# Narrow layers: the rests of two units in one transpose, and an accumulation left open for a step

## The reference

```
q = x @ Wq;  k = context @ Wk;  v = context @ Wv        (B: x * rsqrt(mean(x*x) + eps) * norm_w ahead of Wq)
logits = q k^T * scale (+ column bias in A)
x = x + softmax(logits) @ v @ Wo (+ bo in A)
```

## Time and profile before

| | |
|---|---|
| median of 3 runs (lowest to highest) | 2020.38 us (2019.39 to 2020.8) |
| the profiled execution, own time | 2020.28 us |
| its span | 2018.5 us |
| granted TensorE clock | 1.000 of full speed |
| PE, DVE, ACT, POOL busy | 1993.4, 1434.6, 985.6, 646.2 us |

### The profile page before, as it was taken

One profiled execution on the slowest core, in us unless ns is written; L12 is line 12 of the kernel. 1 busy time (PEld: TensorE's weight loads), 2 busy tenths in 40 slices (PEclk: granted clock), 3 DMA queues, 4 the chain that ended last, 5 costly groups with the idle time before them and its releaser, 6 DMA issues.

```text
span 2018.5 us, 31330 instructions
## 1 busy us (share of the span) xinstructions
PE 1993.4 (99%) x11482; PEld 1738.1 (86%) x11482; DVE 1434.6 (71%) x2488; ACT 985.6 (49%) x1814; POOL 646.2 (32%) x518
## 2 busy tenths in 40 slices
PE   8999999999999999999999999999999999999998
PEld 8999988888888887888888888888888878888887
DVE  4423367777777767888888677776777677888886
ACT  3222255444544554655555454444455555555553
POOL 0000043222222255554444332222222354443441
PEclk9999999999999999999999999999999999999999
DMA  8789742222222223343333332222222232333332
GB/s 236 150 174 212 188 92 63 78 62 62 67 78 63 65 75 96 103 112 98 89 100 96 82 111 66 62 67 78 62 63 70 79 89 72 100 95 87 86 74 85
DMA packets 262538, 191.02 MB, mean 95 GB/s; under 512 B 197522, under 2 KB 199986, under 8 KB 259826
## 3 DMA queue, kind: packets, MB, share of 16 engines
q1 hardware_dynamic: 262386, 189.03, 36.8%
HBM read 132.66 MB, written 56.26 MB: 94 GB/s over the span
## 4 chain that ended last, share of the span: by engine, by line
PE 50%; issue 31%; POOL 13%; DVE 4%; ACT 1%; SPq 0%; DMA 0%; POOLq 0%; DVEq 0%; ACTq 0%
POOL prob L1405 6%; PE acc_bank L900 6%; PE ctx_bank L270 4%; PE t_bank L878 4%; PE ctx_bank L271 4%; PE ctx_bank L272 4%; POOL x_s L1380 4%; PE q_bank L856 3%; PE q_bank L858 3%; PE q_bank L860 3%; PE acc_bank L270 3%; PE acc_bank L272 3%; PE acc_bank L271 3%; PE s_bank L270 2%; POOL rest L1414 2%
## 5 line engine op out<-in xcount | busy, mean ns | idle before, releaser
L1405 POOL TENSOR_TENSOR prob<-prob,rinv 128x1232 f32<-128x1232 f32 x128 | 288.3, 2252 | 1010.4 <-DVE rinv L1255 1010.4
L856 PE MATMUL q_bank<-x_s,w_s 128*128 128x512 f32 x768 | 315.6, 411 | 0.8 <-POOL w_s L1398 0.8
L860 PE MATMUL q_bank<-x_s,w_s 128*128 128x512 f32 x768 | 307.1, 400 | 0.0
L858 PE MATMUL q_bank<-x_s,w_s 128*128 128x512 f32 x768 | 307.0, 400 | 0.0
L270 PE MATMUL acc_bank<-o_s,w_s 128*128 128x512 f32 x752 | 304.5, 405 | 2.2 <-DVE o_s L1246 2.2
L272 PE MATMUL acc_bank<-o_s,w_s 128*128 128x512 f32 x752 | 294.4, 392 | 0.0
L271 PE MATMUL acc_bank<-o_s,w_s 128*128 128x512 f32 x752 | 293.4, 390 | 0.0
L1069 ACT ACTIVATE s_bank<-bias_s 128x308 f32<-128x308 f32 x256 | 109.9, 430 | 361.2 <-DVE prob L1217 361.2
L1213 DVE TENSOR_REDUCE mx<-s_bank 128x4 f32<-128x308 f32 x512 | 241.6, 472 | 61.5 <-PE s_bank L272 49.3
L900 PE MATMUL acc_bank<-pT_s,vals_s 128*128 128x512 f32 x1024 | 280.4, 393 | 3.5 <-DVE pT_s L1232 3.5
L1084 ACT ACTIVATE prob<-prob,rstd 128x308 f32<-128x308 f32 x256 | 141.3, 553 | 279.9 <-DVE prob L1217 251.1
(11 more groups left out here) (107 smaller groups left out, 4136.4 us busy)
## 6 DMA issues: line engine op xcount, KB each, us to landing
stream<-x_back SPq DMA_DIRECT2D x128, 256.0 KB, 2.7
x_front<-stream SPq DMA_DIRECT2D x96, 256.0 KB, 3.4
x_back<-stream SPq DMA_DIRECT2D x96, 256.0 KB, 3.5
kvw_raw<-kvw SPq DMA_DIRECT2D x17, 1024.0 KB, 8.6
k_scr<-k_out SPq DMA_DIRECT2D x36, 308.0 KB, 9.8
keys_s<-k_scr SPq DMA_DIRECT2D x128, 77.0 KB, 2.4
v_scr<-v_out SPq DMA_DIRECT2D x8, 1024.0 KB
vals_s<-v_scr SPq DMA_DIRECT2D x512, 6.5 KB
```

Source lines behind the costliest of these rows:

```text
L856: pe.matmul(out, w[0], x_now[0], start=k == 0, stop=False)
L858: pe.matmul(out, w[0], x_now[1], start=False, stop=False)
L860: mm = pe.matmul(out, w[1], x_now[0], start=False, stop=k == XC - 1)
L1405: pool.tensor_tensor(view, view, rinv[:, slot].unsqueeze(2).broadcast_to([P, TILES * GH, CTX]), ALU.mult).then_inc(p_norm, 1)
```

## The change

It touches the narrow units 32 to 61 and 96 to 125, taken two by two as 15 **pairs** in each narrow layer; the first of a pair is even (`paired_first`).

- POOL copies the rest of every narrow unit into one half of the tile `rest` behind `normalise`, the even unit's into columns 0 to 63, the odd one's into 64 to 127 (one copy a unit that was not there; the even one waits until PE has read the tile). PE transposes both together, four matmuls of 128 columns, in the even step s = odd unit + 1; in the odd step transposes 2 fall away. ACT and DVE split the bank in two instructions each, one for a half. The odd unit's high and low parts lie the other way round on the partitions, and its values are loaded so (`swapped`).
- The even unit's last two value matmuls need that joint transpose, so its accumulation stays open: in the even step only 6 of 8 are run, and the last 2 (`opened`) come in the next, odd step (`closes`), behind the scores of tiles 0 and 1. Values now always use bank 0 and projections bank 1 there.
- In these odd steps PE makes the whole query ahead of the scores of tiles 2 and 3. ACT splits the even unit's output first and the query between the exponentials. DVE splits the even unit's output behind tile 1, then query, transposes 0 and the odd unit's output, and only then makes the softmax sums.

The core of the diff (left out: bank numbers that now come from a table, and counts of semaphores that follow):

```diff
+def swapped(pieces):
+
+    halves = {row: parts for _, _, _, blk, row, parts in pieces if blk == TWICE}
+    return [(h, t0, t1, blk, row, halves[(row + 64) % P] if blk == TWICE else parts)
+            for h, t0, t1, blk, row, parts in pieces]
...
-            values = [("pv", s - 2, m) for m in range(kind(s - 2).Q)] if 0 <= s - 2 < NU else []
+            values = [("pv", s - 3, 0)] if self.closes(s) else []
+            if 0 <= s - 2 < NU and not self.paired_first(s - 2):
+                values += [("pv", s - 2, m) for m in range(kind(s - 2).Q)]
+            if 0 <= s - 1 < NU:
+                turns += [(s - 1, n) for n in range(TWICE + 1) if n < TWICE or not self.paired_first(s - 1)]
...
+        self.turn = {item: n for n, item in enumerate(turns)}
...
+    def paired(self, u):
+
+        return 0 <= u < NU and kind(u).name == "B" and u % UNITS < UNITS - 2
+
+    def paired_first(self, u):
+        return self.paired(u) and u % 2 == 0
+
+    def closes(self, s):
+
+        return self.paired_first(s - 3)
...
-                for h, t0, t1, blk, row, (first, last) in kind(u).pieces:
+                pieces = kind(u).pieces if kind(u).name == "A" or u % 2 == 0 else swapped(kind(u).pieces)
+                for h, t0, t1, blk, row, (first, last) in pieces:
...
-                after(pe, t_lo, 3 * u + n - 1)
+                if (u, n) not in plan.turn:
+                    return
+                item = plan.turn[(u, n)]
+                after(pe, t_lo, item - 1)
                 a = kind(u).name == "A"
-                if n == TWICE and a:
+                if n == TWICE:
                     pe.wait_ge(p_gathered, plan.gathered(u))
                 for t in range(TILES):
                     base = PAIR * n if a else P * n
                     if n < TWICE:
                         rows, p = P, prob[:, u % 2, t, base:base + P]
                     else:
-                        rows, p = (P, rest[:, t]) if a else (64, prob[:, u % 2, t, SC - REST_B:SC])
-                    mm = pe.transpose(t_bank[(3 * u + n) % 2][0:rows, t * P:t * P + P], p, ident[:, :])
+                        rows = P if a or u % 2 else REST_B
+                        p = rest[:, t, 0:rows]
+                    mm = pe.transpose(t_bank[item % 2][0:rows, t * P:t * P + P], p, ident[:, :])
...
-                        pe.wait_ge(t_lo, 3 * u + n + 1)
+                        pe.wait_ge(t_lo, (plan.rest_turn(u) if n == TWICE else plan.turn[(u, n)]) + 1)
                         v = [vals_s[:, u % 2, i, h] for h in range(2)]
                         terms = [(v[0], 2 * n), (v[0], 2 * n + 1), (v[1], 2 * n)]
                         if n == TWICE:
-                            terms = [(v[0], 2 * n + m)] if kind(u).name == "A" else [(v[0], 2 * n), (v[1], 2 * n)]
+                            terms = ([(v[0], 2 * n + m)] if kind(u).name == "A"
+                                     else [(v[0], 2 * n + u % 2), (v[1], 2 * n + u % 2)])
...
                 v = values(s - 2) if 0 <= s - 2 < NU else iter(())
@@ -1013,9 +1068,13 @@
                     half = 12 if s + 1 < NU and kind(s + 1).name == "A" else 6
                     run(scores(s, 0), 1)
                     run(scores(s, 1), 1)
+                    if plan.closes(s):
+                        run(opened, 3)
                     run(q, half)
                     if plan.stats_at(s) is not None:
                         stats(plan.stats_at(s))
+                    if plan.closes(s):
+                        run(q, half)
                     if plan.behind(s):
                         project(*projections.pop(0))
                     run(scores(s, 2), 1)
@@ -1023,7 +1082,11 @@
                     run(v, 3)
                     turned(0)
                     run(q, half)
-                    run(v, 9)
+                    if plan.paired_first(s - 2):
+                        run(v, 3)
+                        opened = v
+                    else:
+                        run(v, 9)
                     turned(1)
                     turned(2)
...
+                elif n == TWICE:
+                    if plan.paired(u) or u % 2 == 0:
+                        e = act.activation(pT_s[0:64, 2 * n], out[0:64, :], ACT.Copy)
+                    if u % 2:
+                        e = act.activation(pT_s[64:P, 2 * n + 1], out[64:P, :], ACT.Copy)
+                else:
...
+                    if plan.closes(s):
+                        split_o(s - 3, 0)
                     if s < NU:
                         exps(s, 0)
+                        if plan.closes(s):
+                            next(q, None)
                         exps(s, 1)
                     bias(s + 1, 0)
                     bias(s + 1, 1)
                     turned(0)
                     next(q, None)
                     next(q, None)
-                    for m in range(pv):
-                        split_o(s - 2, m)
+                    if not plan.paired_first(s - 2):
+                        for m in range(pv):
+                            split_o(s - 2, m)
...
+                    dve.wait_ge(t_mm, plan.turned(u - 2))
+                    if plan.paired_first(u - 2):
+                        dve.wait_ge(p_gathered, plan.gathered(u - 2))
...
-                    dve.tensor_tensor(pT_s[64:P, 2 * n], t_bank[(3 * u + n) % 2][0:64, :],
-                                      pT_s[0:64, 2 * n].bitcast(F32), ALU.subtract).then_inc(t_lo, 1)
+                    if plan.paired(u) or u % 2 == 0:
+                        e = dve.tensor_tensor(pT_s[64:P, 2 * n], out[0:64, :], pT_s[0:64, 2 * n].bitcast(F32),
+                                              ALU.subtract)
+                    if u % 2:
+                        e = dve.tensor_tensor(pT_s[0:64, 2 * n + 1], out[64:P, :],
+                                              pT_s[64:P, 2 * n + 1].bitcast(F32), ALU.subtract)
+                    e.then_inc(t_lo, 1)
...
+                    soon = plan.behind(s) or plan.closes(s)
                     if s < NU:
                         for t in range(TILES):
                             tile_scores(s, t)
-                            if t == 1 and plan.behind(s):
+                            if t == 1 and soon:
                                 for item in plan.late(s - 1):
                                     add_result(*item)
+                            if t == 1 and plan.closes(s):
+                                rest_o(s - 3, 0)
                             if t == 1 and plan.stats_at(s) is not None:
                                 mean_squares(plan.stats_at(s))
-                    if not plan.behind(s):
+                    if not soon:
                         for item in plan.late(s - 1):
                             add_result(*item)
                     if plan.behind(s):
                         add_result(*projections.pop(0))
                         denominators(s)
                         turned(0)
+                    elif plan.closes(s):
+                        next(q, None)
+                        turned(0)
+                        rest_o(s - 2, 0)
+                        denominators(s)
                     else:
                         turned(0)
                         if s < NU:
                             denominators(s)
                     next(q, None)
                     next(q, None)
-                    for m in range(pv):
-                        rest_o(s - 2, m)
+                    if not plan.paired_first(s - 2) and not plan.closes(s):
+                        for m in range(pv):
+                            rest_o(s - 2, m)
...
+                pool.wait_ge(p_norm, u + 1)
+                if u and (kind(u).name == "A" or u % 2 == 0):
+                    pool.wait_ge(t_mm, plan.turn[(u - 1, TWICE)] + 1)
                 if kind(u).name == "A":
-                    pool.wait_ge(p_norm, u + 1)
-                    if u % UNITS:
-                        pool.wait_ge(t_mm, 3 * u)
                     twice = rest[:, :, :].rearrange("q t (w d n) -> q t w d n", w=2, d=2)
                     ends = prob[:, slot].rearrange("q t (w n) -> q t w n", w=2)[:, :, :, PAIR - REST_A:PAIR]
                     for copy in range(2):
                         ins = pool.tensor_copy(twice[:, :, :, copy], ends)
-                    ins.then_inc(p_gathered, 1)
+                else:
+                    half = slice(REST_B * (u % 2), REST_B * (u % 2) + REST_B)
+                    ins = pool.tensor_copy(rest[:, :, half], prob[:, slot, :, SC - REST_B:SC])
+                ins.then_inc(p_gathered, 1)
```

More of the change, by code:

```diff
@@ L129, in __init__ @@
         queries = [("q", 0, m) for m in range(kind(0).Q)]
-        acc = []
+        acc, turns = [], []
         for s in range(STEPS):
@@ L148, in __init__, with by_use, turned, rest_turn @@
         self.acc = {item: n for n, item in enumerate(acc)}
+        self.turn = {item: n for n, item in enumerate(turns)}
+        self.acc_bank, self.acc_before = [], []
+        for n, item in enumerate(acc):
```

(54 more changed lines are left out.)

8 lines of the change are left out of this document (4 added, 4 removed).

## The result

The changed kernel takes 2026.18 us (median of 7 runs, 2025.35 to 2026.56), the kernel before 2020.8 us beside it (7 runs, 2019.39 to 2021.23): ratio 1.0028, 95% interval 1.0016 to 1.0039. It is slower by 0.28%, with an interval that leaves out no change; the forecast was 2025.5 us. The sum came out right, but two of its terms and several places outside it did not; they nearly cancel.

The account below looks back on a forecast made before the run. PE's own list was taken to set the pace in narrow steps, with 0.7 us of slack. The terms -12.0 + 0.9 + 9.8 + 5.0 + 1.4 = +5.1 gave 2025.5 us, with an 8-in-10 range of 2010 to 2036.

Parts of the forecast that it names:

- The gain, -12.0: Narrow pairs: four transposes fewer on PE save 0.43 us in each of 28 pairs, 12.0 us.
- First pairs, +0.9: First pair of each layer: no gain, and two value matmuls moved from step 34 to 35 cost 0.46 us; 0.9 together.
- Waits for the root, +9.8: Even steps behind stats: late root delays exponentials and DVE's split; PE's waits cost 0.7 us, 14 times: 9.8 us.
- the last starts at 5.67: Even steps behind stats: the last of ACT's four exponentials starts 5.67 us into the step, 4.77 before.
- The list of waits that was named as the sign: PE's list of waits: transposes waiting for DVE's split, 10 to 20 us in all in about 14 cases.
- The weight ahead of the root, +5.0: Steps 36, 40, 44 and 100: a quarter of a weight ahead of the root adds 1.26 us each, 5.0 us.
- Scores of tile 3, +1.4: Even steps: PE's scores of tile 3 wait for a later reduction, about 0.05 us in 28 steps: 1.4 us.
- The two terms together: Waits for the root, +9.8 us, and scores of tile 3, +1.4 us, in the even narrow steps.
- 6 x 0.235: Odd steps: half a query placed ahead of tiles 2 and 3 makes them later by 1.41 us.
- Covered waits: Rival: the wait for the root stays covered, 2010.6 us if nothing waits; chances 0.16 nearly whole gain, 0.2 half.
- An open accumulation that comes late: Rival: DVE delays the open unit's matmuls, 0.4 us in each of 30 odd steps, 2037.5 us; chance 0.12.
- The clock: Rival: PE's waits in four steps lower its clock to 1.2 GHz, 10 us more each, 2065 us; chance 0.02.

Follow-up runs that it names:

- e10: Changed kernel with root first, query half before wide units back behind the scores, accumulation banks exchanged, pairs from the third unit on: 2010.59 us, ratio 0.9946 to before.
- e1: Changed kernel with POOL's root issued ahead of `normalise` in narrow steps with stats: 2013.97 us, ratio 0.9965 to the kernel before.
- e7: Changed kernel with POOL's root ahead of the quarter of weights, still behind normalisation and copy: 2021.79 us, ratio 1.0003 to the kernel before.
- e5: Changed kernel with root first and, ahead of a wide unit, the second half of the query back behind the scores: 2012.32 us, ratio 0.9956 to before.
- e9: e5 with the two accumulation banks exchanged in narrow layers (value sums bank 1, projections bank 0): 2011.04 us, ratio 0.9951 to the kernel before.
- e3: Changed kernel with DVE's sums and reciprocal ahead of the query and output splits again in odd steps: 2047.78 us, ratio 1.0133 to the kernel before.
- e4: e1 plus query half behind scores ahead of a wide unit, and alternating bank for the first projection of steps 34 and 98: 2014.28 us, ratio 0.9965.
- e6: e5 with the pairs beginning two units later in each narrow layer: 2011.67 us, ratio 0.9959 to the kernel before.

## Why the prediction was right, point by point

**The gain, -12.0: right.** A plain pair saves 0.44 us where 0.43 was reckoned from the earlier trace rows. By the figure of the Trainium skill that was weighed there (TensorE: Matmul & The Clock Gate, "Back-to-back issue gap") it would have been an estimated 0.32; the measurement stands with the row.

**First pairs, +0.9: right in size.** e10 leaves them out and wins 0.51 us a layer, two value matmuls. They fall due at the layer's end, where the last pair closes.

**Waits for the root, +9.8: the mechanism right, the size too big.** 14 x 0.53 = 7.4. The first exponential was forecast 4.03 us into the step and came 961.62 - 957.63 = 3.99. The step that failed is the next one, "the last starts at 5.67", which adds's 1.64 us for three exponentials in a row. That row holds a wait: the third one could start only when DVE's subtraction was done, at 913.83 + 0.48 = 914.31, while the first two, 1.00 us together, stood some 0.45 apart. Lines of the kernel before, ACT and DVE:

```profile
913.25 1.00 ACT L1084 ACTIVATE prob<-prob,rstd 128x308 f32<-128x308 f32 x2 [4.12 <-POOL rstd L1419]
914.34 0.55 ACT L1084 ACTIVATE prob<-prob,rstd 128x308 f32<-128x308 f32 x1
...
913.83 0.48 DVE L1217 TENSOR_TENSOR prob<-s_bank,mx 128x308 f32<-128x308 f32 x1
```

In the changed kernel all four are ready when the root comes. They take 1.88, so they start 0.44 apart and the last one 1.33 after the first, not 1.64. DVE's split was due at 6.73 and came at 6.38. In e1 the whole term goes. The list of waits that was named as the sign came out in number and not in make-up: 9.9 us on PE, but in nine cases and four of them the root's; the 14 cases stand in PEld's list.

**The weight ahead of the root, +5.0: right.** 4 x 1.25; e7 takes away 4.4 us by itself, 4.9 by the same steps of the profiled executions.

**Scores of tile 3, +1.4: not there.** The plain pair saves all it should.

**The two terms together** are 3.8 us too large, and the steps from 35 to 62 and from 99 to 126 came out 3.5 us below their forecast, 0.7 against 4.2. About as much, 3.3 us, came from steps 34, 63 and 127, which the sum had at nothing or at 0.5 each. That the total came so near is therefore in part luck: two errors of like size and opposite sign.

- *Step 63, +1.85 against +0.5.* The half query between the scores was weighed as "6 x 0.235", but ahead of a wide unit a half is 12 matmuls. DVE's split comes late and transposes 2 of unit 62, which has no partner, wait 1.32 us. e5 puts that right for 1.5 us; the rest is the last pair's moved matmuls.

```profile
1126.16 0.63 PE L929 MATMUL t_bank<-ident,rest 128*64 128x128 f32 x4 [1.32 <-DVE pT_s L1326]
```

- *Step 34, +1.2 against nothing.* The prediction left out the banks. With sums in one and projections in the other, the first projection of step 34 gets the bank where step 33's late one still stands. In layer 3 the alternation happens to leave it free. e9 shows it by mending it.

```profile
805.76 0.50 PE L316 MATMUL acc_bank<-o_s,w_s 128*128 128x512 f32 x1 [0.93 <-DVE x_back L1361]
```

- *The end, +1.2 against +0.5.* 0.5 are the moved matmuls, 0.4 a longer wait in step 127 (0.58 us; 0.17 before, the last line here). The last 0.3 were not tested: a wait of 0.56 us that names no releaser stands where the bank of the closing sum would have to be free.

```profile
1994.20 0.93 PE L953 MATMUL acc_bank<-pT_s,vals_s 128*128 128x512 f32 x3 [0.56 <-issue]
...
1997.75 0.63 PE L929 MATMUL t_bank<-ident,rest 128*64 128x128 f32 x4 [0.58 <-DVE pT_s L1326]
...
1991.63 0.63 PE L878 MATMUL t_bank<-ident,prob 128*64 128x128 f32 x4 [0.17 <-DVE pT_s L1240]
```

- *Up to step 32, +0.8.* The profiled execution of the changed kernel is that much late from unit 0 on; e1's is 0.3 and e3's 1.1 us earlier than it at the same place. All three carry the same code up to there, so that is the spread of one execution and no effect of the edit.

**The rivals.** Covered waits: e1 is the run in which the 14 waits are gone and nothing else is moved, and it takes 2014.0 us, not the 2010.6 of that case; that e10 reaches this number, with the borders mended and the pairs begun later, is chance. An open accumulation that comes late: in no odd step of the changed kernel (10.35 us against 10.42), though it did in e4 and e6 through its bank. The clock: a granted clock of 1.0 in all seven executions of the changed kernel.

## What to carry to other kernels

When a step is moved on one engine, list everything that stands behind its consumer on the next one: here the sums went some 2 us later on DVE in the steps with stats (`normalise` from 1.73 us ahead of the step's end to 957.90 - 957.63 = 0.27 behind it), and what cost time was a root on POOL that needs neither sums nor copy and only stood last. Put such a small result ahead of the long work as soon as its input is there; in the kernel before that would have won nothing, so the place to look for it is in the changed order, not in the old profile. And work out the first, last and border steps of a pattern by themselves: here the 56 steady steps were forecast 3.5 us too high, and steps 34, 63 and 127 together 3.3 us too low.

## What the runs showed of the hardware

A single gap on PE can cost the clock, or not. In e4, PE stood still for 2.2 us and soon after ran at a granted clock of 0.50 for some 3 us, and step 34 grew by 1.75 us, where the gap is only 1.28 longer than the wait of 0.93 us that it replaced. In e6 a gap of 2.1 us, two steps on, left the clock full in the profiled execution; the same windows there:

```profile
830.00:831.00 1.00, 0.06 (x1) 0.10 (x1) 0.83 (x2) 0.55 (x1) 0.00 (x0) 1.00 0.63 173
831.00:832.00 1.00, 1.00 (x6) 0.83 (x7) 0.00 (x0) 0.00 (x0) 0.00 (x0) 1.00 0.30 56
832.00:833.00 1.00, 1.00 (x7) 0.86 (x6) 0.03 (x1) 0.60 (x1) 0.00 (x0) 1.00 0.44 143
```

Nor is it the same in every execution of one kernel. Of e4's five, four had a mean granted clock of 0.999, and the one with 1.000 was the fastest, 2012.51 us against the median's 2014.28. Of e6's five, one had 0.998 and took 2015.69 us, where the median is 2011.67; where in it the clock fell no trace shows. In the changed kernel, gaps of up to 1.5 us in the narrow layers (the waits for `o_s` in the list above) left the clock full. Why one gap cost the clock and another did not stays open. The Trainium skill (TensorE: Matmul & The Clock Gate, "HAM oscillation") tells of a clock that falls when TensorE waits for data between stretches of matmuls, in a kernel whose waits are longer than these. In e4's trace a shorter gap was enough, in a kernel whose TensorE is busy 99% of the span; in e6's it was not.

Activations on 128x308 that stand one behind another start 0.44 us apart though each lasts 0.55 (four in 1.88 us at 961.62 in the changed kernel): the duration in a row is not the distance.
